# One order of work for all images of an attention block: all sixteen score tiles first, then the attend of the image in front, v, and the image's own first attend

## The reference

```
h   = group_norm(x)                     # 32 groups of 8 channels, eps 1e-5
q, k, v = h @ Wq + bq, h @ Wk + bk, h @ Wv + bv
s   = (q @ k^T) * 256**-0.5             # 1024 x 1024 for each image
out = x + (softmax(s) @ v) @ Wo + bo
```

## Time and profile before

| | |
|---|---|
| median of three runs | 1806.69 us |
| the profiled execution: its time | 1806.59 us |
| its span, from the first to the last instruction | 1804.9 us |
| TensorE matmuls busy | 1797.8 us |
| VectorE busy | 1666.2 us |
| ScalarE busy | 985.8 us |

### The profile page before, as it was taken

How to read it: one execution, slowest core, us unless ns; L and a number is a source line. 1 busy time by engine, 2 the same in 40 slices (tenths; PEclk the granted TensorE clock), 3 DMA queues, 4 the chain that set the end, 5 groups by cost and what they waited for, 6 DMA issues and landing times.

```text
span 1804.9 us, 32681 instructions
## 1 busy us (share of the span) xinstructions
PE 1797.8 (100%) x11589; PEld 1642.2 (91%) x11589; DVE 1666.2 (92%) x2922; ACT 985.8 (55%) x1355; POOL 91.2 (5%) x106
## 2 busy tenths in 40 slices
PE   9999999999999999999999999999999999999999
PEld 8989999899898999998999989999899898999989
DVE  7999999999999999999999999999999999999997
ACT  5565554654655646556455465554654645646554
POOL 0000000000000000000000000000000000000000
PEclk9999999999999999999999999999999999999999
DMA  3222122221222211222212222132321223211201
GB/s 117 59 71 61 21 70 58 70 70 29 52 59 69 70 40 41 67 61 70 57 24 70 58 70 60 21 70 58 70 69 28 54 58 70 70 40 41 68 14 36
DMA packets 28809, 101.92 MB, mean 56 GB/s; under 512 B 3189, under 2 KB 3962, under 8 KB 28794
## 3 DMA queue, kind: packets, MB, share of 16 engines
q0 software_dynamic: 9072, 33.03, 12.0%
q1 hardware_dynamic: 19722, 68.69, 11.7%
HBM read 68.16 MB, written 66.58 MB: 75 GB/s over the span
## 4 chain that ended last, share of the span: by engine, by line
PE 95%; DVE 3%; issue 1%; DMA 0%; ACT 0%; POOL 0%; SPq 0%; DVEq 0%; POOLq 0%
PE ps_s L856 47%; PE ps_o L950 13%; PE ps_o L951 13%; PE ps_o L952 13%; PE ps_o L856 9%; DVE s_buf L620 1%; DMA s_buf<-in_L_conv_Wk_dram 0%; DVE top L590 0%; DVE h_lo L563 0%; DVE p_lo L628 0%; DVE o_buf L640 0%; DVE g_lo L570 0%; DVE bn_parts L495 0%; POOL group_stats L298 0%; DVE query_max L607 0%
## 5 line engine op out<-in xcount | busy, mean ns | idle before, releaser
L950 PE MATMUL ps_o<-v_rows,p_hi 128*128 128x258 f32 x2048 | 577.9, 282 | 0.0
L952 PE MATMUL ps_o<-v_rows,p_lo 128*128 128x258 f32 x2048 | 576.1, 281 | 0.0
L951 PE MATMUL ps_o<-v_lo,p_hi 128*128 128x256 f32 x2048 | 575.8, 281 | 0.0
L349 ACT ACTIVATE p_hi<-s_buf 128x1024 fp32r<-128x1024 f32 x256 | 272.2, 1063 | 509.2 <-DVE s_buf L620 509.2
L856 PE MATMUL ps_s<-g_hi,h_hi 128*128 128x512 f32 x1024 | 399.6, 390 | 1.5 <-DVE g_lo L570 1.5
L856 PE MATMUL ps_s<-g_hi,h_lo 128*128 128x512 f32 x1024 | 399.2, 390 | 0.0
L856 PE MATMUL ps_s<-g_lo,h_hi 128*128 128x512 f32 x1024 | 398.8, 389 | 0.0
L950 PEld LDWEIGHTS ps_o<-v_rows,p_hi 128*128 128x128 f32 x2048 | 385.9, 188 | 2.4
L951 PEld LDWEIGHTS ps_o<-v_lo,p_hi 128*128 128x128 f32 x2048 | 384.8, 188 | 2.9
L952 PEld LDWEIGHTS ps_o<-v_rows,p_lo 128*128 128x128 f32 x2048 | 384.6, 188 | 0.0
L341 ACT ACTIVATE s_buf<-ps_s 128x512 f32<-128x512 f32 x512 | 293.0, 606 | 161.0 <-PE ps_s L856 158.5
(11 more groups left out here) (95 smaller groups left out, 2194.9 us busy)
## 6 DMA issues: line engine op xcount, KB each, us to landing
x_t<-in_x_turned_dram SPq DMA_DIRECT2D x64, 512.0 KB, 4.0
out_dram<-in_x_dram SPq DMA_DIRECT2D x63, 512.0 KB, 7.2
out_dram<-o_buf POOLq DMA_DIRECT2D x63, 512.0 KB, 5.4
x_last<-in_x_dram SPq DMA_DIRECT2D x1, 512.0 KB, 7.9
out_dram<-o_buf SPq DMA_DIRECT2D x4, 128.0 KB, 1.9
s_buf<-in_L_conv_Wq_dram SPq DMA_DIRECT2D x1, 256.0 KB, 5.5
s_buf<-in_L_conv_Wk_dram SPq DMA_DIRECT2D x1, 256.0 KB, 5.8
s_buf<-in_L_conv_Wv_dram SPq DMA_DIRECT2D x1, 256.0 KB, 6.0
```

What stands on the lines that cost most here:

```text
L349: nc.scalar.activation(p_hi[c][:, rows, :], s_buf[c][:, rows, :], ACT.Exp, scale=SCALE).then_inc(p_hi_done, 1)
L950: nc.tensor.matmul(ps[:, 0:VC], p_hi[c][:, m, cols], v_hi[:, m, :], start=m == 0, stop=False)
L951: nc.tensor.matmul(ps[:, VC - C:VC], p_hi[c][:, m, cols], v_lo[:, m, :], start=False, stop=False)
L952: last = nc.tensor.matmul(ps[:, 0:VC], p_lo[c][:, m, cols], v_hi[:, m, :], start=False, stop=m == T - 1)
```

## The change

TensorE's order is now the same for all images: scores of both halves (sixteen tiles), attend of half 1 of the image in front, v, attend of half 0, g of the next image. `project_v` waits for all sixteen copies (`project_v(b, 16)`), the first attend takes v and p piece by piece (`attend(b, 0, j, True)`), and `h_parts(b + 1)` waits for v instead of the scores, since v now reads h last. The lists of the other engines follow: ScalarE copies eleven score tiles, then puts one further copy behind each pair of exponentials; VectorE has the next image's statistics between the maxima of half 0, and the maxima of half 1 between the pieces of half 0. On GpSimd `inverse_std` goes ahead of `store(b - 1, 1)`. The first image loses its own order of v parts. The core of the diff:

```diff
@@ gpsimd @@
             with pool.Fori(1, B - 1) as b:
+                inverse_std(b + 1)
                 store(b - 1, 1)
-                inverse_std(b + 1)
                 store(b, 0)
@@ scalar @@
             def h_parts(b):
-                act.wait_ge(s_ps, b * 16)
+                act.wait_ge(v_ps, b * 4)
...
+            def scores_and_first_softmax(b):
                 for m in range(T):
                     scores_out(b, 0, m)
+                for m in range(3):
                     scores_out(b, 1, m)
                 for i in range(NP):
                     exponentials_hi(b, 0, i)
                     exponentials(b, 0, i)
                     scores_out(b, 1, 3 + i)
                 scores_out(b, 1, 7)
                 for i in range(4):
                     v_part(b, i)
+            def second_softmax(b, project):
+                for i in range(2):
                     exponentials_hi(b, 1, i)
                     exponentials(b, 1, i)
+                for i in (2, 3):
+                    exponentials_hi(b, 1, i)
+                    project(2 * i - 4)
+                    exponentials(b, 1, i)
+                    project(2 * i - 3)
+            def image(b):
+                scores_and_first_softmax(b)
+                h_parts(b + 1)
+                second_softmax(b, lambda i: g_part(b + 1, i))
@@ vector @@
+            def first_softmax(b):
+                part_maxima(b, 0)
+                query_maxima(b, 0)
+                row_maxima(b, 0)
+                difference(b, 0, 0)
+                difference(b, 0, 1)
+                maxima(b, 1, 0)
+                difference(b, 0, 2)
+                difference(b, 0, 3)
+                p_rest(b, 0, 0)
+                maxima(b, 1, 1)
+                p_rest(b, 0, 1)
+                maxima(b, 1, 2)
+                p_rest(b, 0, 2)
+                maxima(b, 1, 3)
+                p_rest(b, 0, 3)
+                maxima(b, 1, 4)
+            def second_softmax(b, h_next, project):
+                difference(b, 1, 0)
+                h_next(0)
+                difference(b, 1, 1)
+                h_next(1)
+                finish(b, 0, 0)
+                difference(b, 1, 2)
+                p_rest(b, 1, 0)
+                finish(b, 0, 1)
+                difference(b, 1, 3)
+                p_rest(b, 1, 1)
+                finish(b, 0, 2)
+                project(0)
+                finish(b, 0, 3)
+                project(1)
+                p_rest(b, 1, 2)
+                project(2)
+                project(3)
+                p_rest(b, 1, 3)
+            def middle(b):
+                for j in range(TQ):
+                    finish(b - 1, 1, j)
+                v_rest(b, 0)
+                part_maxima(b, 1)
+                for i in (1, 2, 3):
+                    v_rest(b, i)
+                query_maxima(b, 1)
+                row_maxima(b, 1)
+            def image(b):
+                channel_stats(b + 1)
+                dve.wait_ge(bn_done, b * 4 + 8)
+                maxima(b, 0, 0)
+                next_sums(b)          # channel_sums, group_means, group_spread
+                maxima(b, 0, 1)
+                group_variance(b + 1)
+                maxima(b, 0, 2)
+                turn_back(b + 1)
+                maxima(b, 0, 3)
+                normalise(b + 1)
+                maxima(b, 0, 4)
+                first_softmax(b)
+                middle(b)
+                second_softmax(b, ...)
@@ tensor @@
-            body: scores(b, 0, m) x8; attend(b - 1, 1, j) x4; project_v(b); scores(b, 1, m) x8;
-                  attend(b, 0, j) x4; project_g(b + 1)
+            def image(b, first=False):
                 for m in range(T):
                     scores(b, 0, m)
                 for m in range(T):
                     scores(b, 1, m, True)
+                if not first:
+                    for j in range(TQ):
+                        attend(b - 1, 1, j)
+                project_v(b, 16)
+                for j in range(TQ):
+                    attend(b, 0, j, True)
+            image(0, True)
+            project_g(1)
             with pe.Fori(1, B - 1) as b:
+                image(b)
+                project_g(b + 1)
+            image(B - 1)
+            for j in range(TQ):
+                attend(B - 1, 1, j, last_block=True)
```

More of the change, by code:

```diff
@@ L705, in first_image @@
                 row_maxima(0, 0)
[L706 to L717 removed]
+                for i in range(NP):
+                    difference(0, 0, i)
+                for i in range(NP):
+                    p_rest(0, 0, i)
+                for i in range(4):
+                    v_rest(0, i)
                 for step in range(5):
                     maxima(0, 1, step)
[L720 to L723 removed]
                 part_maxima(0, 1)
@@ L726, in first_image @@
                 row_maxima(0, 1)
-                g_rest(1, 0)
-                difference(0, 1, 0)
-                g_rest(1, 1)
-                difference(0, 1, 1)
-                g_rest(1, 2)
-                g_rest(1, 3)
-                difference(0, 1, 2)
-                p_rest(0, 1, 0)
-                difference(0, 1, 3)
-                finish(0, 0, 2)
-                p_rest(0, 1, 1)
-                finish(0, 0, 3)
-                p_rest(0, 1, 2)
-                maxima(1, 0, 0)
@@ L771, in scores_first @@
-            def scores_first(b):
-                for step in range(5):
-                    maxima(b, 0, step)
-            def body(b):
-                def next_stats():
-                    channel_stats(b + 1)
-                    dve.wait_ge(bn_done, b * 4 + 8)
-                softmax_beside(b, 0, lambda j: finish(b - 1, 1, j), nothing, lambda i: v_rest(b, i),
-                               next_stats, lambda: channel_sums(b + 1))
-                group_means(b + 1)
-                group_spread(b + 1)
-                maxima(b, 1, 0)
+                second_softmax(0, lambda k: h_rest(1, k), lambda i: g_rest(1, i))
@@ L786, in body @@
                 group_variance(b + 1)
-                maxima(b, 1, 1)
+                maxima(b, 0, 2)
                 turn_back(b + 1)
-                maxima(b, 1, 2)
+                maxima(b, 0, 3)
                 normalise(b + 1)
-                maxima(b, 1, 3)
-                maxima(b, 1, 4)
-                softmax_beside(b, 1, lambda j: finish(b, 0, j), lambda k: h_rest(b + 1, k),
-                               lambda i: g_rest(b + 1, i), nothing, nothing)
+                maxima(b, 0, 4)
@@ L796, in last_image @@
+                first_softmax(b)
+                middle(b)
+                second_softmax(b, lambda k: h_rest(b + 1, k), lambda i: g_rest(b + 1, i))
             def last_image(b):
@@ L840, in _ @@
             first_image()
-            body(1)
-            with dve.Fori(2, B - 1) as b:
-                scores_first(b)
-                body(b)
+            with dve.Fori(1, B - 1) as b:
+                image(b)
             last_image(B - 1)
@@ L906, in project_g, with project_v @@
                                              for a, h in ((a_hi, h_hi), (a_hi, h_lo), (a_lo, h_hi))], g_ps)
-            def project_v(b, scores_done=8, first=False):
-                for i in FIRST_V if first else range(4):
-                    if first and i >= 2:
-                        pe.wait_ge(s_out, i + 5)
-                    elif i < 2:
+            def project_v(b, scores_done):
+                for i in range(4):
+                    if i < 2:
                         after(pe, o_out, b * 8 + (i + 1 - 4))
@@ L984, in _ @@
             pe.wait_ge(fold_done, 2)
-            def body(b, first=False):
-                for m in range(T):
-                    scores(b, 0, m)
-                if not first:
-                    for j in range(TQ):
-                        attend(b - 1, 1, j)
-                project_v(b, first=first)
-                for m in range(T):
-                    scores(b, 1, m, first_v=first)
-                for j in range(TQ):
-                    attend(b, 0, j)
-                project_g(b + 1)
-            def last_image(b):
+            def image(b, first=False):
                 for m in range(T):
```

196 lines of the change are left out of this document (20 added, 176 removed).

## The result

The changed kernel takes 1941.08 us (median of four runs, 1939.29 to 1941.92) against 1806.88 us: ratio 1.0743, 95% interval 1.073 to 1.0757. The forecast was 1896.0, with a range to 1920. The direction was right; 45 us were missing, and the time lies outside the range. The profiled execution has a span of 1940.2 us where the forecast's sum was 1894.3. (TensorE's clock doesn't fall in the same images in every execution, so medians and single profiles can differ by 1 to 2 us.)

A forecast was written before the change was run, and what follows sets the result against it. TensorE's matmuls bound the kernel before, at 55.75 us an image; the new period was put at 58.33. Span 1804.9 + 9.8 (first image) + 77.4 (30 steps) + 2.2 (last image) = 1894.3, plus 1.7 gives 1896.0 us; range 1860 to 1920.

The forecast's parts named there:

- The ring and its pause: Dependency loop v, row maximum, softmax, next row maximum, exponential, copy, sixteenth tile, attend, v; TensorE waits 2.3 us at that tile.
- Statistics and maxima of half 0, the power: VectorE's next-image statistics and half 0 maxima; GpSimd's power (for inverse_std) beside a 512-column maximum leaves 0.6 us wait open.
- V: Start of an image's v on TensorE in steady state; first difference of half 0 forecast 41.56 us behind it.
- the ring's other part: From the first difference of half 0 to the next v: 16.77 us, taken whole from the last image before.
- the row bears out no such lock: Claim that GpSimd's power and a two-SBUF-input VectorE maximum run side by side at usual lengths, despite the skill's exclusive port lock.
- Rival B: Power on GpSimd and VectorE's 0.57 us maximum run one after the other: 17 us more, 1913; chance 0.05.
- rival C: TensorE's clock falls in the pauses, slowing the attend behind each: 86 us more, 1982; chance 0.04.
- First image: First scores of image 1 at 74.3 us instead of 64.51, since g waits for the second `h_rest`: +9.8 us.
- Last image: Row maximum of half 1 behind the v parts makes the last pieces of p late for the attend: +2.2 us.
- The issue pauses: 2.8 us of TensorE "issue" pauses, placed in the old trace's middle; left in the sum.

The follow-up runs named there:

- e2: Changed kernel with six unused 128-column matmuls and their weight loads on TensorE ahead of the sixteenth score tile; 1916.75 us, ratio 1.061.
- e3: Changed kernel with ScalarE's copies of half 1's score tiles 3 to 5 ahead of the first exponential, 6 and 7 behind the first two pairs; 1836.53 us.
- e5: Changed kernel with VectorE's row maximum of half 1 ahead of all four v parts instead of behind them; 1925.05 us, ratio 1.066.
- e1: Changed kernel with the next image's variance, and so the power, one maximum earlier, ahead of half 0's second maximum; 1905.54 us, ratio 1.0547.
- e7: Changed kernel with the third maximum of half 0 behind `turn_back`, so nothing lies beside the power; 1957.94 us, ratio 1.0831.
- e4: Kernel before with only the changed kernel's first image, all further images as before; 1816.42 us, ratio 1.0053.
- e11: e9 plus own first-image order on ScalarE and VectorE; in the last image, VectorE's half 1 row maximum ahead of v parts, two differences between them; 1808.76 us.
- e6: e5 with the statistics' sums, variance and power ahead of the maxima of half 0, plus one tiny VectorE maximum; 1926.88 us, ratio 1.0668.
- e9: Changed kernel with the edits of e3 and e1, and the first two g parts ahead of the last two finishes; 1814.63 us, ratio 1.0048.

## Why the prediction was wrong

The sum was 1894.3 and the span is 1940.2: +45.9. Two of its steps failed. The largest term is one that the forecast put at nothing: TensorE's clock behind the pause that the forecast itself contained, 24.5 us. The other is the power on GpSimd, priced as if the maximum beside it cost it nothing: 0.47 us a step, 14 us. Without the clock's falls the time would lie inside the range: e2, which keeps the clock up, takes 1916.75 us, where the range ends at 1920. By the prediction's own steps:

**The ring and its pause** were right. The pause is at the sixteenth tile, ended by the copy, 2.58 us for 2.3; 0.2 for g; 1.42 for the copy at the first maximum of half 1; v parts. From the first difference (994.53) to the next v (1011.26) it is 16.7 us, with 16.77 forecast. e3 shows that this ring is what the pause hangs on. It was incomplete: I named the ring over v alone, and e5 points to another over g, only 0.5 us shorter. That didn't change the forecast, but it would have spoilt any remedy built on it.

**Statistics and maxima of half 0, the power: wrong.** 41.56 from V to the first difference came out as 994.53 - 952.25 = 42.28, and with the ring's other part the step is 0.68 longer than forecast, 20.4 us. 0.47 of it is the power, which takes 1.50 instead of 1.03: from the maximum beside it to `turn_back` it is 1.69 us (985.71 to 987.40) and not 1.22. Some 0.1 lies in the waits for score tiles (0.56 and 0.13 us for 0.6 in all), 0.1 between `turn_back` and the row maximum (2.98 us for 2.90), and the rest in gaps under 0.05. The failing sentence is "the row bears out no such lock". In the earlier trace rows the power started at 940.29 and the maximum at 940.33, so the power was first. In the new order the maximum is first by 0.08. The trace of before held the other case too, once among 32 (GpSimd, then VectorE):

```profile
158.88 2.06 POOL L298 TENSOR_TENSOR group_stats<-g_var,minus_half 128x4 f32<-128x4 f32 x1 [9.44 <-DVE g_var L535]
...
158.81 1.23 DVE L590 TENSOR_TENSOR top<-top,s_buf 128x1024 f32<-128x1024 f32 x1
161.04 0.24 DVE L540 STREAM_TRANSPOSE norm<-group_stats 128x64 f32<-128x64 f32 x1 [1.00 <-POOL group_stats L298]
```

I had read the usual row and not the exception. Rival B had the mechanism with the wrong victim: here the maximum isn't delayed, the power is (e1 and e7). The Trainium skill, page "SBUF — State Buffer", section "SBUF: two separate sides", says that whichever starts first has the ports for its whole instruction. By that rule the power behind a maximum comes late, and here it does (1.50, 2.06); the other way round, a maximum started 0.04 us behind the power should be held as well, and the earlier trace rows show it isn't (in 28 of 32 images of before the maximum starts 0.03 to 0.04 us behind and keeps its 1.23).

**The clock (rival C, chance 0.04, priced at 86 us): it happened, with the price too high and the chance too low.** It costs 1.53 us in 16 of 30 images, 24.5 us. On the chance: I noted that no pause of before was as long as the forecast's own 2.3 us, so its trace couldn't speak for a clock that stays up, and I still gave the likeliest case a full clock. A term of unknown size belonged in the range. e2 removes it alone: 24.3 us. Why it falls in one image and not in the next, at equal pauses, stays open.

**First image: +3.65 us** (77.95 for 74.3), and mostly the clock once more. The third v bank starts at 48.58, with 48.4 forecast. But at the granted clock of 0.50 it and the fourth take some 2.6 us each and not 1.40, so the row maximum of half 1 is ready at 64.17 instead of 61.3. The 12.2 us from there to the second g part hold to the digit (76.38). The last 0.8 is g, which ends later than its second part is made: it starts at 69.63 and not at 65.9, because `project_g` needs `finish(0, 0, 0)`. I let it start with the second `h_rest` and overlooked the finish behind it. It would still have been done by the second g part, had it not run at half the clock: 8.3 us from its start to the first scores, where the earlier trace rows have 5.45. Against the earlier trace rows the first image loses 13.4 us; by e4 10 of some 12 stay.

**Last image:** +2.6 with 2.2 forecast, right. e11 supports the named cause: with the row maximum ahead of the v parts (and two differences between them) the last image is back to 0.4 us over before.

**The issue pauses** of the earlier trace rows are not in the trace's middle, as I had it: they lie at first scores of images 1 to 3, and before's first steps are 57.12 and 56.90 us for 55.75. I left them in the sum, and the new kernel doesn't have them there: the 30 steps of before take 1675.1 us in all, 2.6 more than 30 x 55.75 = 1672.5, so -2.6. Together 3.65 + 20.4 + 24.5 + 0.4 - 2.6 = 46.4, where 45.9 are to be explained.

## What to carry to other kernels

When work on one engine is moved to one place, look for the lists beside it that fed its pauses: here five score copies put earlier on ScalarE, an engine half idle, were worth 105 us, 24.5 us of clock among them. Where the forecast itself contains a pause that the old trace doesn't have, the old trace says nothing of the clock behind it, and the range must. Of a row that shows two engines side by side without loss, read which started first, and look for the rare row where it was the other.

## What the runs showed of the hardware

- A GpSimd instruction of 1.03 us that starts 0.06 to 0.15 us behind a VectorE maximum with two SBUF operands ends 0.89 us behind that maximum's end: 1.50 us beside 512 columns, 2.06 beside 1024 (1.97 in e6, where the maximum is 0.15 us ahead). If it starts 0.04 us ahead, both keep their length.
- TensorE's granted clock fell from 2.4 to 1.2 GHz behind pauses that came once an image: in 5 of 30 images with pauses of 1.9 us (e1), 16 of 30 with 2.6, 21 of 30 with 2.9 (e7), in none of the 30 with e2's matmuls in the pause. Each fall cost some 1.5 us. The Trainium skill, page "TensorE: Matmul & The Clock Gate", section "What's actually happening", tells of a clock gate set by how busy TensorE has been of late, and e2 agrees with it: added work in the pause alone keeps the clock.
- One pause of TensorE shows in two rows of the waits: 0.2 us of the matmul for g, and 0.6 us of "issue" of its weight load (17.4 us over 29 images), which starts 0.01 us ahead of that matmul instead of some 0.2. When e5 and e9 took the wait away, both went.
